# Second attention: the weighted sum directly behind the second scores, the four first scores of a step as one run

## What is computed

```python
q, k, v = split(x @ qkv_w + qkv_b)                     # 16 heads of 8
k_enh = k + kv_gate * gram_gate * k_geo                # prepared ahead: KS4
v_enh = v + kv_gate * gram_gate * v_geo                # prepared ahead: V9
scores = jnp.einsum('bhtd,bhsd->bhts', q, k_enh) * SCALE
scores = jnp.where((diffs >= 0)[None, None], scores, -jnp.inf)
attn = jax.nn.softmax(scores, axis=-1)
out = jnp.einsum('bhts,bhsd->bhtd', attn, v_enh)
```

## Time and profile before

| | |
|---|---|
| median of 3 executions | 1227.88 us (1225.12 to 1231.95) |
| the profiled execution | 1228.41 us, span 1226.4 us, mean granted clock 0.917 of full |
| busy share of the span | PE 83%, DVE 62%, ACT 49%, POOL 27% |
| passes 0 to 85 of `attention_b` | 834.65 to 1088.95 us |

### The profile page before, as it was taken

How to read it: one execution, slowest core, us unless ns; L and a number is a source line. 1 busy time by engine, 2 the same in 40 slices (tenths; PEclk the granted TensorE clock), 3 DMA queues, 4 the chain that set the end, 5 groups by cost and what they waited for, 6 DMA issues and landing times. The chain is left out here.

```text
span 1226.4 us, 18761 instructions
## 1 busy us (share of the span) xinstructions
PE 1021.1 (83%) x6414; PEld 642.7 (52%) x6414; DVE 757.9 (62%) x1957; ACT 603.2 (49%) x1177; POOL 329.4 (27%) x418
## 2 busy tenths in 40 slices
PE   4489999999989999999727478789999999996273
PEld 2357666666657666666426353344554454534263
DVE  5167765776576756677512579788777777755222
ACT  2376666666576656666202145234555545564020
POOL 0432112211122112210043205353443343321332
PEclk9699999999999999999958678899999999998577
DMA  5620000000000000000142100000000000002322
GB/s 176 165 58 1 2 1 1 1 2 1 1 1 1 1 1 1 1 1 1 46 136 62 52 1 1 1 1 1 1 2 1 2 1 1 2 1 58 122 61 88
DMA packets 47614, 32.39 MB, mean 26 GB/s; under 512 B 9104, under 2 KB 43680, under 8 KB 47520
## 3 DMA queue, kind: packets, MB, share of 16 engines
q1 hardware_dynamic: 45472, 26.93, 7.8%
q0 software_dynamic: 2048, 4.26, 1.0%
HBM read 21.59 MB, written 11.69 MB: 27 GB/s over the span
## 5 line engine op out<-in xcount | busy, mean ns | idle before, releaser
L713 DVE TENSOR_REDUCE attn_b_least<-attn_b_slot 128x1 f32<-128x512 f32 (+3 forms) x384 | 194.5, 553 | 59.7 <-PE attn_b_slot L631 40.3
L444 ACT ACTIVATE attn_a_prob<-attn_a_score,attn_a_m_all 128x128 f32<-128x128 f32 (+7 forms) x256 | 189.2, 739 | 74.3 <-DVE attn_a_m_all L366 70.5
L780 ACT ACTIVATE attn_b_probT<-attn_b_st 128x1024 f32<-128x1024 f32 (+1 forms) x192 | 145.2, 808 | 145.8 <-PE attn_b_st L655 144.4
L362 DVE TENSOR_REDUCE attn_a_m_far<-attn_a_score 128x1 f32<-128x512 f32 (+3 forms) x192 | 105.8, 551 | 94.9 <-PE attn_a_score L276 92.6
L300 PE MATMUL attn_a_o<-attn_a_ptsb,Vd 128*64 128x512 f32 x288 | 154.3, 618 | 0.0
L300 PE MATMUL attn_a_o<-attn_a_ptsa,Vd 128*64 128x512 f32 x288 | 154.2, 617 | 0.0
L288 PE MATMUL attn_a_slot<-tab,attn_a_prob 128*128 128x128 f32 x1152 | 149.7, 274 | 0.0
L629 PE MATMUL attn_b_slot<-KS,attn_b_alone 128*128 128x512 f32 (+2 forms) x384 | 142.2, 437 | 4.1 <-POOL attn_b_alone L802 2.1
L288 PEld LDWEIGHTS attn_a_slot<-tab,attn_a_prob 128*128 128x128 f32 x1152 | 132.3, 141 | 11.0 <-issue 2.4
L629 PEld LDWEIGHTS attn_b_slot<-KS,attn_b_alone 128*128 128x128 f32 x384 | 71.1, 196 | 86.2 <-DVE attn_b_least L713 54.2
L453 ACT ACTIVATE attn_a_ptsa<-attn_a_slot 128x512 f32<-128x512 f32 x144 | 85.8, 596 | 58.1 <-PE attn_a_slot L288 57.6
(11 more groups left out here) (235 smaller groups left out, 1912.7 us busy)
## 6 DMA issues: line engine op xcount, KB each, us to landing
moe_weights_w<-in_L_ffn_w_dram SPq DMA_DIRECT2D x32, 256.0 KB, 5.1
to_experts<-xn SPq DMA_DIRECT2D x2, 1056.0 KB, 9.2
moe_experts_xe<-to_experts SPq DMA_DIRECT2D x16, 132.0 KB, 2.7
bias_by_query_and_key<-bias_by_distance SPq DMA_DIRECT2D x2, 1024.0 KB
bias_near<-bias_by_query_and_key SPq DMA_DIRECT2D x2, 1024.0 KB, 8.0
from_experts<-xn SPq DMA_DIRECT2D x2, 1024.0 KB, 9.8
moe_experts_back<-from_experts SPq DMA_DIRECT2D x8, 256.0 KB, 3.6
moe_weights_b<-in_L_ffn_b_dram SPq DMA_DIRECT2D x16, 64.0 KB, 5.5
```

What stands on the lines that cost most here:

```text
L362: nc.vector.tensor_reduce(least, score[t % 2][:, 0:nk - win], AX.X, ALU.min).then_inc(far_done, 1)
L444: nc.scalar.activation(probs(g)[:, j, 0:nk], score[t % 2][:, 0:nk], ACT.Exp, bias=m_all[:, j:j + 1], scale=-1.0, accum_out=rowsum[g % 2][: ...
L713: nc.vector.tensor_reduce(least[m // PER % 2][:, c, a, qt:qt + 1], bank[u % SLOTS_S][:, 0:w], AX.X, ALU.min).then_inc(slot_free, 1)
L780: nc.scalar.activation(probT[n % 2][:, two, lo:], st[:, two, lo:], ACT.Exp, scale=-1.0).then_inc(exp_done, 1)
```

## The change

In a pass of the PE program the weighted sum moves ahead of all four first scores; before, it stood between the second and the third. No instruction is added or removed, and the programs of the other engines stay as they are.

```diff
                     shifts_t(n, 0)
                     shifts_t(n, 1)
-                if ahead:
-                    scores(m, 0)
-                    scores(m, 1)
                 if 0 <= n - 1 < STEPS:
                     values(n - 1)
                 if ahead:
-                    scores(m, 2)
-                    scores(m, 3)
+                    for a in range(GRP):
+                        scores(m, a)
                 if turns_max(n) is not None:
```

## The result

The change made the kernel slower, by about as much as forecast: 1254.66 us median (1246.41 to 1256.92, 4 executions) against 1229.91 us (1225.12 to 1233.26, 4 executions), a ratio of 1.0189 with a 95% interval of 1.0141 to 1.0237. A second measurement of the same kernel gave 1249.8 us and a ratio of 1.0175 (1.0115 to 1.0235). The ratios are those on record, with their intervals; the medians divided give 1.020 and 1.0145. Single slow executions, the longest 1501.22 us of the kernel before and 4423.83 us of `planned`, are left out of every ratio. The forecast was 1246 us, 1.5% slower, with a range of 1237 to 1256.

A forecast was written before the change was run, and what follows sets the result against it. PE's own instruction stream was taken to set the pace. Seven times 2.55 us for twelve passes, plus 0.39 for pass 85, gave 18.2 us on 1228.4: 1246.6 profiled, median 1246 us, range 1237 to 1256.

The forecast's parts named there:

- PE sets the pace: From 834 to 1089 us PE is busy 254.69 of 255 us, so its own instruction stream sets the pace.
- The ring binds: In a plain pass the fourth fill waits for the first fill's slot: 1.71 us against 1.32, +0.39 us.
- The terms of the other passes: Per pass: turn of cols +0.74, diagonal 512 +0.39, 384 +0.10, 256 +0.09, 128 -0.04 or 0, hidden +0.01 and 0 us.
- the cover of 0.11 us: In pass 25, POOL and ACT finish 0.11 us before the moved weighted sum's place; costed at nothing.
- the terms of the turns: Passes with a turn: +0.74 us for plain with cols, +0.39 each for diagonal 512 with OT.
- The hidden passes: n modulo 12 = 0 and 4: exponentials hold them at about 2.76 us, so they lose 0.01 and 0 us.
- The late weighted sum as a rival: If POOL builds masked queries before zeroing, one pass of twelve waits about 1 us: 7 us more, 1253; chance 0.06.
- one of the prediction's own signs of being wrong: The prediction called itself wrong if L670, the weighted sum, shows idle time behind POOL L816.
- A change of tiling costs 0.08 us: Four tiling changes in a pass become three; by that rule alone 85 passes would gain 6.8 us.
- The first rival: Ring does not bind, one tiling change fewer gains 6 to 13 us, to about 1219; chance 0.04.
- the stretch that the prediction named as a sign: The prediction called itself wrong if the clock falls between 834 and 1100 us.
- the clock rival: PE pauses drop the stage's clock to 0.90, so its 255 us grow by about 25: 1271; chance 0.05.

The follow-up runs named there:

- planned: Kernel before, with four pairs of passes holding their eight first fills as three and two, then three and none; 1227.86 us, ratio 0.9975.
- short_before: Kernel before, with each DVE reduction reading only the first 64 columns of its bank; 1229.14 us, ratio 0.9981.
- short_after: Changed kernel, with each DVE reduction reading only the first 64 columns of its bank; 1217.03 us, ratio 0.9862.
- three_one: Kernel before, with the weighted sum moved between the third and the fourth first score; 1238.66 us, ratio 1.0045.
- planned_b: Kernel before, with pairs n modulo 12 = 4 and 5, 8 and 9, 10 and 11 holding three and two, then three and none; 1224.28 us, ratio 0.9927.
- one_three: Kernel before, with the weighted sum moved between the first and the second first score; 1240.44 us, ratio 1.0069.

## Why the prediction was right, point by point

- **PE sets the pace, and the listed wait of L629 for DVE was not a real one.** Right: in short_before DVE's reductions take 0.22 us instead of up to 0.69, and passes 1 to 85 didn't get shorter (252.56 against 251.92 us). The listed wait didn't shrink either: 52.2 us in 845 to 1080 us, where it was 46.2. It says nothing on the pace here.
- **The ring binds once the weighted sum is gone from between, 0.39 us in a plain pass.** Right to 0.01 us, read from pass 0 at 1.71 us. Shown to be the cause by short_after, which keeps everything else.
- **The terms of the other passes.** Each within 0.03 us, but for 0 and 1 together, 0.49 instead of 0.40. There the weighted sum met POOL's zeroing and ACT's copy: the cover of 0.11 us was too thin (the weighted sum starts 0.14 us after the end of the copy), and by the estimate above 0.06 us were lost where the prediction took nothing and bounded it at 0.1. The pair 4 and 5 was 0.03 over. In sum 19.4 us instead of 18.2: the terms of the turns and of these two passes were mis-sized, each by hundredths.
- **The hidden passes.** Right for 24, whose 0.36 us came back in the next one almost in full. For 4 the loss of 0.11 us shows in the pass and is given back by the next. The sign "passes 16 and 24 still about 2.76 us long" holds for 24 (2.74 us) but not for 16, which went from 2.52 to 2.63 us.
- **The late weighted sum as a rival**: it happened, at 0.06 us in one pass of twelve, not at 1 us. The trace puts seven waits of L670's weight load, 1.8 us in all, down to POOL. That is one of the prediction's own signs of being wrong, and it did appear; its size is what the prediction bounded. POOL kept its order.
- **A change of tiling costs 0.08 us.** The rule of the Trainium skill, TensorEngine Tiling (Array Packing), section Key Properties, that a change of tiling mode drains TensorE, has the right sign when the slots are there: 7.1 us in 85 passes, 0.083 us each. But short_after saves a group of fills together with the change of tiling, and no run parts the two, so the equal size may be chance. As a forecast for this kernel the rule would have been wrong by 26 us.
- **The first rival's threshold.** It was put too late: the prediction wanted the fourth slot about 1.0 us behind the first fill, and a reduction 0.3 us shorter. In short_after the fourth fill follows the third by 0.25 us and starts at 0.82, so the 1.28 us would have to fall by about 0.46.
- **PE's busy time** was to be unchanged or lower. It rose by 5.2 us, from 251.92 to 257.11; why is not worked out.
- **The clock.** It did not fall between 843.64 and 1114.92 us, in the passes of the change. But from 834.00 to 843.64 us it was at 0.50, the lower level, within the stretch that the prediction named as a sign; pass 0 took 3.46 us there instead of 2.38. The whole start of the stage ran at 0.60 once, and at 0.78 with the same kernel again; the kernel before had 0.85. Its order in that stretch is the one of before, and no run shows that the change plays any part in it. The price of the clock rival was also a little low: 255 us at 0.90 are 283, 28 us more and not 25.
- **Why the median lies 8.7 us over the point.** The profiled execution lies 6.3 us over its own forecast of 1246.6: 1.2 us from the terms, 4.0 from the later begin of the stage, 2.6 from its start, less 1.6 at its end. The other 2.4 us are how far executions lie apart. The median is 1.3 us below the upper end of the range, and two of the four executions lie above it; that it stayed inside is in part luck, while the 19.4 us for 18.2 are not. The second measurement was 3.8 us over.

## What to carry to other kernels

What stands between two uses of a ring is its cover, even where the busy engine never stands idle: before an instruction is moved away, look for a place where the ring's users already stand without it. Here one such place, pass 0, gave the price to a hundredth of a microsecond. Count every user of the ring, the rare ones too: in the runs of three it was the turn's slot, not the fills', that came late, and the expectations of three_one and planned had overlooked it. Fewer groups of fills are worth having (3.2 us in planned_b), each no longer than the ring allows.

## What was not expected of the hardware

A third fill in a row adds 0.23 us (three fills and what follows in 0.89 us, 928.32 to 929.21 above), where two in a pair take 0.66, 0.33 each: each group pays about 0.2 us once. The pairs 4 and 5, 8 and 9 of planned_b, with one group fewer, gained 0.24 and 0.21 us. A fourth fill adds 0.36 us even in short_after (1.25 less 0.89), and there the group fewer gave only 0.08 us. That the 0.2 us are the group's first load and its change of tiling is likely, but no run measured it by itself. And the start of the stage took between 22.93 and 26.96 us over the kernels whose reductions are whole, at granted clocks from 0.85 (before) to 0.57 (planned, whose start holds one fill more). The same program in it, in the changed kernel's two profiles, took 25.55 us at 0.60 and 23.54 us at 0.78; one_three, with the order of before in that stretch, took 26.21 us at 0.57. That is over 3 us in which the kernel's order has no part.
